# Twenty turns written out, and idle matmuls ahead of ten steps of a two-layer adaLN kernel

## The chip, the cores and the metric

The kernel runs on one core of one Trainium2 chip. The metric is the device time in microseconds (us) of one execution. Three executions without a profiler took 1416.13, 1418.07 and 1418.85 us; the median is 1418.07. All tensors are fp32.

## The reference

The input `x` is 32 sequences of 256 tokens with 128 channels. Two layers follow each other. Each has six modulation vectors per sequence, `silu(c) @ wmod`, and wraps an attention-like block and a feed-forward block:

```
h = layernorm(x) * (1 + ca) + sa ;  x = x + ga * attn(h)
h = layernorm(x) * (1 + cb) + sb ;  x = x + gb * ffn(h)
```

In layer 0 `attn` is linear attention over 32 heads of 4 channels with rotary angles: two decaying states S and K per head are updated token by token (`S = S*beta + phi_k v`, `K = K*beta + phi_k`), the output is a softmax-weighted sum of `phi_q S / (phi_q K + eps)`, then an output product, a residual and a layer norm. In layer 1 `attn` is an RWKV block: layer norm, a shift by one token, key, value and receptance products, a numerically guarded WKV recurrence over the tokens, an output product, and a channel mix (products to 512 channels, relu squared, back to 128, gated). `ffn` in both layers quantizes its input, its weights and its hidden values to FP4 in blocks of 16, and computes `silu(x Wg) * (x Wu)` with 352 hidden channels and the product back to 128.

## The kernel before

The 32 sequences go through as 16 pairs (`PAIRS`); a pair is 512 tokens, four tiles of 128 rows (`NT`). The work of a pair is cut into steps: `a1` to `a8` for the attention of layer 0, `b1` to `b6` for the feed-forward of either layer, `c1` to `c8` for layer 1's attention. A software pipeline runs over turns. In turn n every engine works on pair n (first norm), pair n-1 (layer 0 attention), pair n-2 (layer 0 feed-forward and the first norm of layer 1), pair n-3 (layer 1 attention) and pair n-4 (layer 1 feed-forward). There are 20 turns; turns 0 to 3 fill the pipeline and turns 16 to 19 drain it. The order of the steps within a turn is a list written out by hand for each engine in its `body(n)`. Engines meet through semaphores, and each engine's queue is in order.

The turns are run by the helper `turns` (line 342). Turns 0 to 5 are written out, turns 6 to 15 are a register loop of five iterations with two bodies in each (line 346), and turns 16 to 19 are written out again. Inside the loop the turn number is a register.

Results of TensorE go to eight banks of PSUM. The table `BANK` gives each step's result its bank, so several steps share one. Before a step writes, it waits until the reader of what last stood there is done. The helper `freed` waits for that; `freed_at_ends` waits only when the turn is a plain number, which means that its waits are there in the written-out turns and absent in the loop, where other waits imply them. After these waits a step waits for its data (`after`, `wait_ge`).

Steps that matter below, with the lines of their instructions: `a4d` (L968) sums query times key state into `a_den`; DVE reads it at L1595, inverts it and multiplies in the mix; `a5` (L989) spreads the result over the rows, into the same bank; DVE takes it at L1608 and multiplies the states by it at L1588; `a4` (L977) sums those. `a6` is L1000 and L1001. `b1T_0` and `b1T_1` are transposes through the helper `turn` (L904), as is `c2`; `rows_back` is L1038; `b2` transposes the quantized input (L1096); `b3_0` and `b3_1` are the gate and up products (L1101), in the first use behind the turning of the weights (`turn_weights`, L893 and L897); `b5_0` and `b5_1` transpose the hidden values (L1180) and `down` (L1213) multiplies them. `c3` is L1250 and L1251, `c5` L1271 and L1272, `c6` L1303.

In the profile one fp32 matmul of the program is two records, so `x2` is one matmul.

Of the kernel before, what the change touches and what calls it, by code (L numbers as in the profile page):

```python
# [24 lines left out]
NB, T = 32, 256  # L25
SEQ = 2
TOK = SEQ * T
NT = TOK // P
PAIRS = NB // SEQ
# [63 lines left out]
def after(eng, sem, turn, per_turn=1, nth=None):  # L93

    eng.wait_ge(sem, turn * per_turn + (per_turn if nth is None else nth))
# [16 lines left out]
def freed(eng, sem, turn, per_turn=1, nth=None):  # L112

    if isinstance(turn, int):
        if turn < 0:
            return
        turn = min(turn, PAIRS - 1)
    after(eng, sem, turn, per_turn, nth)


def freed_at_ends(eng, sem, turn, per_turn=1, nth=None):

    if isinstance(turn, int):
        freed(eng, sem, turn, per_turn, nth)
# [12 lines left out]
def build(nc, a, scratch, out):  # L137
    ctx = ExitStack()
    with ctx:
        def sb(name, shape):  # L140
            return ctx.enter_context(nc.sbuf_tensor(name, shape, F32))

        def sem(name):
            return ctx.enter_context(nc.semaphore(name))


        const = sb("const", [P, CONST.shape[1]])

        def cst(k):
            return const[:, CONST_AT[k][0]:CONST_AT[k][1]]  # L150

        ident, center = cst("ident"), cst("center")
# [106 lines left out]
        def bank(name):  # L259
            return ps[:, BANK[name], :]  # L260
# [30 lines left out]
        s_kscan, s_qk_sum, s_den = sem("key_scan"), sem("q_key_sum"), sem("den_mm")  # L291
        s_share, s_shch, s_share_mm, s_qsh = sem("share"), sem("chain_share"), sem("share_mm"), sem("share_times_query")
# [12 lines left out]
        s_fq = [sem(f"ffn_xq{l}") for l in range(2)]  # L305
# [14 lines left out]
        s_wch, s_wexp_in, s_wexp, s_wy = sem("chain_wkv"), sem("wkv_exponents"), sem("wkv_exps"), sem("wkv_y")  # L320
# [20 lines left out]

        def turns(eng, body):

            for n in range(6):
                body(n)
            with eng.Fori(3, PAIRS // 2) as m:
                body(2 * m)
                body(2 * m + 1)
            for n in range(PAIRS, PAIRS + 4):
                body(n)  # L350


# [1 line left out]
        def _(sp):  # L354
# [30 lines left out]
            def body(n):  # L385
                do(load_x, n)
            turns(sp, body)
            for p in range(2):
                sp.wait_ge(s_out[p], 8 * PAIRS)
# [3 lines left out]
        def _(pool):  # L393
# [59 lines left out]
            def body(n):  # L453
# [5 lines left out]
                do(power_a1, n - 2)  # L459
                do(power_a0, n)  # L460
            turns(pool, body)


        @block.scalar
        def _(act):
# [394 lines left out]
            def store(j):  # L860
                act.wait_ge(s_x4, j + 1)
                dst = out_v[j, :, :, :] if isinstance(j, int) else out_v[bass.ds(j, 1), :, :, :].squeeze(0)
                act.dma_start(dst, of_pair(xb, j)).then_inc(s_out[j % 2], 16)
            s.preload_act_table_set("silu_and_others")
            turns(act, body)


        @block.tensor
        def _(pe):
            t_ = nc.tensor  # L870
            n = [0]
# [6 lines left out]
            for l in range(2):  # L878
                for k in range(6):
                    last = t_.matmul(ps_set[l][:, 2, k * NB:(k + 1) * NB], wmod[:, l, k * H:(k + 1) * H], cT[:, l, :],  # L880
                                     start=True, stop=True)
# [7 lines left out]
            def turn_weights(l):  # L889
# [8 lines left out]
                last.then_inc(s_wT, 1)  # L898
                pe.wait_ge(s_wcp, 3 * l + 3)

            def turn(src, dst, ln, i):
                for t in range(NT):
                    after(pe, s_norm[ln], i, NT, t + 1)
                    last = t_.transpose(dst[:, t * P:(t + 1) * P], src[:, t, :], ident)  # L904
                last.then_inc(s_normT[ln], 1)

            def a1(i):
                freed(pe, s_hqc[0], i - 2, 2, 2)
                freed_at_ends(pe, s_outer, i - 1, 2, 2)
                turn(norm[0], bank("a_nT"), "a0", i)  # L910
# [49 lines left out]
                last.then_inc(s_bm_mm, 1)  # L960

            def a4d(i):
                pe.wait_ge(s_qk_sum, i + 1)
                freed(pe, s_hqc[1], i - 3, 2, 2)
                freed_at_ends(pe, s_phi, i, 2, 2)
                for q in range(SEQ):
                    for m in range(M):
                        last = t_.matmul(bank("a_den")[q * 64:(q + 1) * 64, 0:T], cst(f"sel_den{m}"),  # L968
                                         state[:, m, D, q * T:(q + 1) * T], start=(m == 0), stop=(m == M - 1))
                last.then_inc(s_den, 1)  # L970
# [8 lines left out]
                last.then_inc(s_num, 1)  # L979

            def a5(i, q):
                pe.wait_ge(s_share, i + 1)
                if q == 0:
                    freed(pe, s_gd[0], i - 1, SEQ)
                    freed_at_ends(pe, s_shch, i, 2, 1)
                else:
                    freed(pe, s_bm_th, i, 3, 3)
                for m in range(M):
                    last = t_.matmul(bank(f"a_s{q}")[:, m * T:(m + 1) * T], cst(f"spread{m}")[q * 64:(q + 1) * 64, :],  # L989
                                     share[q * 64:(q + 1) * 64, :], start=True, stop=True)  # L990
                last.then_inc(s_share_mm, 1)
# [12 lines left out]
            def a7(i):  # L1004
                freed(pe, s_x4, i - 3)
                freed_at_ends(pe, s_outer, i, 2, 2)
                freed_at_ends(pe, s_hid[0], i - 1, NT, 4)
                freed_at_ends(pe, s_cch, i - 2)
                turn(zn, bank("a_zT"), "z0", i)
# [16 lines left out]
            def b1T_0(i):  # L1026
                freed(pe, s_th[1], i - 2, NT, 3)
                freed_at_ends(pe, s_u, i, SEQ)
                turn(hq[0], bank("f0_nT"), "f0", i)

            def b1T_1(j):
                freed(pe, s_ag, j, SEQ)
                turn(hq[1], bank("f1_nT"), "f1", j)

            def rows_back(l, i):
# [49 lines left out]
                add_columns(bank("c_x3"), acol).then_inc(s_x3mm, 1)  # L1085

            def b2(l, i):
                pe.wait_ge(s_fq[l], i + 1)
                if l == 0:
                    freed(pe, s_hid[1], i - 2, NT, 4)  # L1090
                    freed_at_ends(pe, s_outer, i + 1, 2, 1)
                else:
                    freed(pe, s_yc, i + 2)
                    freed_at_ends(pe, s_hqc[1], i - 1, 2, 1)
                for t in range(NT):
                    last = t_.transpose(bank(f"f{l}_qT")[:, t * P:(t + 1) * P], hq[l][:, t, :], ident)  # L1096
                last.then_inc(s_fqT[l], 1)
# [77 lines left out]
            def hidden_T(l, i, k):  # L1175
                pe.wait_ge(s_hq[l], i + 1)
                for c, (r0, rn) in enumerate(KC):
                    for t in range(2):
                        col = (c % 2) * T + t * P
                        last = t_.transpose(bank(f"f{l}_h{k}{'aac'[c]}")[0:rn, col:col + P], hid[l][:, 2 * k + t, r0:r0 + rn], ident)  # L1180
                last.then_inc(s_hqT[l], 1)
# [13 lines left out]
            def b5_1(j, k):  # L1195
                if k == 0:
                    freed(pe, s_th[0], j + 2, NT, 4)
                    freed_at_ends(pe, s_norm["c1"], j + 1, NT)
                    freed_at_ends(pe, s_th[1], j, NT, 4)
                    freed(pe, s_hid[0], j + 2, NT, 3)  # L1200
                    freed_at_ends(pe, s_fqc[1], j)
                else:
                    freed(pe, s_fth, j + 1)
                    freed_at_ends(pe, s_th[1], j, NT, 1)
                    freed(pe, s_phi, j + 3, 2, 2)
                    freed_at_ends(pe, s_hid[1], j, NT, 2)
                hidden_T(1, j, k)
# [35 lines left out]
            def c2(j):  # L1243
                freed(pe, s_xn[1], j - 1)
                freed_at_ends(pe, s_qsh, j + 1, SEQ, 1)
                turn(norm[1], bank("c_mT"), "b1", j)

            def shifted(dst, k, src):
# [14 lines left out]
                shifted(bank(f"c_{'kvr'[k]}"), k, xs[0]).then_inc(s_kvr, 1)  # L1263

            def c5(j):
                pe.wait_ge(s_wy, j + 1)
                freed(pe, s_th[1], j - 1, NT, 4)
                freed_at_ends(pe, s_outer, j + 2, 2, 1)
                for t in range(NT):
                    dst = bank("c_x")[:, t * P:(t + 1) * P]  # L1270
                    t_.matmul(dst, wy[:, t * P:(t + 1) * P], w_oc[:, :], start=True, stop=False)  # L1271
                    last = t_.matmul(dst, hcol[1][:, t * P:(t + 1) * P], center, start=False, stop=True)  # L1272
                last.then_inc(s_xm_mm, 1)
# [43 lines left out]
            def body(n):  # L1317
# [11 lines left out]
                do(c5, n - 3)  # L1329
                do(c7x, n - 3)  # L1330
                do(layer(b2, 0), n - 2)
                do(b3_0, n - 2, 0)
                do(b3_0, n - 2, 1)
# [12 lines left out]
                do(c6b, n - 3)  # L1346
                do(b5d_1, n - 4, 1)
                do(a4d, n - 1)
                do(c7, n - 3)
                do(b6r_1, n - 4)  # L1350
# [5 lines left out]
                do(b6x_0, n - 2)  # L1356
                do(b6r_0, n - 2)
                do(a5, n - 1, 0)
                do(a5, n - 1, 1)
                do(b1T_1, n - 3)  # L1360
                do(a4, n - 1, 0, 0)
                do(a4, n - 1, 0, 1)
# [528 lines left out]
```

## Time and profile before

| | |
|---|---|
| median of three executions | 1418.07 us (1416.13 to 1418.85) |
| profiled execution, its own time | 1419.27 us |
| its span, first to last instruction | 1417.1 us |
| TensorE busy (PE) | 1199.9 us, 85% |
| DVE busy | 1123.0 us, 79% |
| ACT busy | 1062.4 us, 75% |
| mean granted TensorE clock | 0.928 |
| DMA | 9 GB/s over the span |

The span is cut in 40 slices of 35.4 us in the page; its clock line has one digit for each, in tenths of the full 2.4 GHz. The clock has two levels, 1.2 and 2.4 GHz, so a digit between them is a mean. The idle time in brackets behind an instruction is that of its engine just before it, with what ended it.

### The profile page before, as it was taken

The numbers are of one execution on the slowest core, as the hardware profiler recorded it, in microseconds if no ns is written. First come the engines' busy times: TensorE is split into PE (matmuls) and PEld (weight loads), VectorE is DVE, ScalarE is ACT, GpSimd is POOL, SyncE is SP. The second block draws the span as 40 slices with busy tenths as digits, with TensorE's granted clock in tenths as the row PEclk, the third lists the DMA queues.
The fourth block names the chain that finished last, engine by engine and source line by source line (L and its number), as shares of the span: only waits on it lengthen the run. The fifth ranks groups of instructions, "written<-read, shape, count | busy, mean of one in ns | idle before, by whom it ended". The sixth has DMA issues, their size and how long they took to land.

```text
span 1417.1 us, 19485 instructions
## 1 busy us (share of the span) xinstructions
PE 1199.9 (85%) x5610; PEld 723.4 (51%) x5610; DVE 1123.0 (79%) x1619; ACT 1062.4 (75%) x2849; POOL 219.3 (15%) x286
## 2 busy tenths in 40 slices
PE   5465888989899998989898988999898989978664
PEld 2133364655555564646455554646465555546443
DVE  5838587979889797979798897979698898964523
ACT  5252868789797978797897979797888979687553
POOL 1000203021211212030212111020212121110000
PEclk9576998999999999999999999999899999999686
DMA  4000000000000000000000000000000000000000
GB/s 130 0 1 8 1 3 6 2 15 1 15 1 16 1 15 2 8 8 0 16 0 15 0 15 1 15 0 8 9 0 15 0 15 1 8 1 8 1 8 7
DMA packets 21486, 13.45 MB, mean 9 GB/s; under 512 B 1552, under 2 KB 20624, under 8 KB 21392
## 3 DMA queue, kind: packets, MB, share of 16 engines
q1 hardware_dynamic: 12944, 8.29, 1.9%
q10 hardware_dynamic: 8448, 4.20, 1.0%
q14 instruction: 70, 0.57, 0.1%
q8 instruction: 24, 0.39, 0.1%
HBM read 8.28 MB, written 4.19 MB: 9 GB/s over the span
## 4 chain that ended last, share of the span: by engine, by line
PE 63%; ACT 14%; DVE 12%; issue 8%; POOL 2%; SPq 0%; ACTq 0%; DMA 0%; DVEq 0%; POOLq 0%
PE ps L1101 11%; PE ps L1213 6%; PE ps L1310 4%; PE ps L924 4%; PE ps L1303 4%; PE ps L1180 3%; PE ps L1012 3%; PE ps L1016 3%; PE ps L1250 3%; PE ps L904 3%; PE ps L1251 2%; ACT hq L507 2%; PE ps L977 2%; PE ps L938 2%; POOL rstd_of_a L416 2%
## 5 line engine op out<-in xcount | busy, mean ns | idle before, releaser
L1101 PE MATMUL ps<-wguT,hqcol 128*128 128x352 f32 x512 | 175.4, 485 | 20.5 <-ACT hqcol L681 12.5
L1562 DVE TENSOR_TENSOR_SCAN state<-beta,outer 128x512 f32<-128x512 f32 x128 | 149.2, 1206 | 0.0
L1101 PEld LDWEIGHTS ps<-wguT,hqcol 128*128 128x128 f32 x512 | 97.0, 199 | 82.1 <-issue 30.8
L423 POOL TENSOR_TENSOR var_of_f<-squares_f,eps_sum 128x4 f32<-128x4 f32 x32 | 11.9, 373 | 670.2 <-ACT hq L507 670.2
L1412 DVE SCALAR_TENSOR_TENSOR hid<-hidcol,hid 128x1408 f32<-128x1408 f32 (+1 forms) x68 | 106.2, 1566 | 7.7 <-ACT hidcol L698 7.6
L1213 PE MATMUL ps<-hidcol,wdT 128*128 128x256 f32 (+1 forms) x384 | 94.2, 390 | 0.0
L1634 DVE TENSOR_TENSOR hid<-th,ps 128x352 f32<-128x352 f32 x128 | 63.4, 512 | 32.1 <-PE ps L1101 19.6
L904 PE MATMUL ps<-const,hq 128*128 128x128 f32 x128 | 35.2, 347 | 54.2 <-ACT hq L497 53.3
L977 PE MATMUL ps<-state,const 128*32 128x512 f32 x256 | 73.4, 867 | 7.7 <-DVE state L1588 7.4
L1588 DVE TENSOR_TENSOR state<-state,qshare 128x1024 f32<-128x1024 f32 x64 | 76.8, 1222 | 2.2
L705 ACT ACTIVATE hidcol<-ps 128x512 f32<-128x512 f32 x64 | 38.1, 595 | 51.9 <-PE ps L1180 51.9
L689 ACT ACTIVATE th<-ps 128x352 f32<-128x352 f32 x128 | 58.9, 460 | 24.2 <-PE ps L1101 21.4
L1213 PEld LDWEIGHTS ps<-hidcol,wdT 128*128 128x128 f32 (+1 forms) x384 | 71.6, 196 | 8.9 <-ACT hidcol L707 0.2
L640 ACT ACTIVATE gcol<-ps,mod_cols 128x256 f32<-128x256 f32 x64 | 26.8, 470 | 61.7 <-PE ps L1213 61.2
L1412 DVE SCALAR_TENSOR_TENSOR hq<-xmag,hq 128x512 f32<-128x512 f32 x64 | 44.3, 692 | 33.7 <-ACT xmag L693 31.4
L1180 PE MATMUL ps<-const,hid 128*128 128x128 f32 (+1 forms) x384 | 55.3, 283 | 18.3 <-DVE hid L1413 17.1
L924 PE MATMUL ps<-rope,wqk 128*64 128x512 f32 x256 | 64.5, 626 | 1.7 <-DVE rope L1542 1.7
L1180 PEld LDWEIGHTS ps<-const,hid 128*128 128x128 f32 (+1 forms) x384 | 44.8, 141 | 38.7 <-issue 37.3
L1250 PE MATMUL ps<-xs,w_mixed 128*128 128x512 f32 x96 | 54.4, 650 | 10.3 <-ACT xs L712 10.3
L1303 PE MATMUL ps<-xk,fw_key 128*128 128x512 f32 x128 | 62.6, 602 | 0.0
L1310 PE MATMUL ps<-fw_val,ex 128*128 128x128 f32 x512 | 61.4, 278 | 1.3 <-ACT ex L760 1.3
L1310 PEld LDWEIGHTS ps<-fw_val,ex 128*128 128x128 f32 x512 | 58.4, 192 | 7.3 <-issue 5.0
(234 smaller groups left out, 3246.9 us busy)
## 6 DMA issues: line engine op xcount, KB each, us to landing
xa<-in_x SPq DMA_DIRECT2D x16, 256.0 KB, 2.7
out<-xb ACTq DMA_DIRECT2D x16, 256.0 KB, 2.2
const<-in_const SPq DMA_DIRECT2D x1, 848.0 KB, 6.8
state<-in_wmod SPq DMA_DIRECT2D x1, 768.0 KB, 4.6
outer<-in_wqk SPq DMA_DIRECT2D x1, 256.0 KB, 4.7
ex<-in_w_gate_up SPq DMA_DIRECT2D x2, 128.0 KB, 3.0
fw_key<-in_fw_key SPq DMA_DIRECT2D x1, 256.0 KB, 2.9
fw_val<-in_fw_val SPq DMA_DIRECT2D x1, 256.0 KB, 3.7
```

Source lines behind the costliest of these rows:

```text
L904: last = t_.transpose(dst[:, t * P:(t + 1) * P], src[:, t, :], ident)
L924: ins = t_.matmul(dst[f * 64:(f + 1) * 64, :], wqk[:, k, f, :], rope[:, 2 * f + n_, :], start=(n_ == 0), stop=(n_ == 1))
L977: last = t_.matmul(bank("a_n")[c * NH:(c + 1) * NH, :], cst("sel_num"), state[:, m, c, :], start=(m == 0), stop=(m == M - 1), tile_positio ...
L1101: t_.matmul(bank(f"f{l}_{'gu'[g]}{t}")[:, 0:I_FF], hqcol[l][:, t * P:(t + 1) * P], wguT[:, l, g, :], start=True, stop=True).then_inc(s_gu[ ...
L1180: last = t_.transpose(bank(f"f{l}_h{k}{'aac'[c]}")[0:rn, col:col + P], hid[l][:, 2 * k + t, r0:r0 + rn], ident)
L1213: last = t_.matmul(bank(f"f{l}_d")[:, toks], wdT[0:rn, l, c, :], hidcol[l][0:rn, c, toks], start=(c == 0), stop=(c == 2))
L1250: t_.matmul(dst, w_mixed[:, k, 0, :], src[:, :, 1:T + 1], start=True, stop=False)
L1303: t_.matmul(bank(f"c_f{c}"), fw_key[:, c * P:(c + 1) * P], xk[:, :], start=True, stop=True).then_inc(s_fk_mm, 1)
L1310: last = t_.matmul(bank("c_vk")[:, t * P:(t + 1) * P], fkr[:, c, t * P:(t + 1) * P], fw_val[:, c, :], start=(c == 0), stop=(c == F4 // P - 1))
L1412: return v.scalar_tensor_tensor(dst, mag, low, dst, ALU.max, (ALU.add, ALU.subtract)[part])
L1562: return v.tensor_tensor_scan(state[:, m, c, :], beta[:, m, :], src, 0.0, ALU.mult, ALU.add)
L1588: v.tensor_tensor(state[:, m, 2 * h:2 * h + 2, :], state[:, m, 2 * h:2 * h + 2, :], qshare[:, m:m + 1, :].to_broadcast([P, 2, TOK]), ALU.m ...
```

## The change

The loop of `turns` is replaced by twenty written-out bodies, so the turn number is a plain number everywhere, and `freed_at_ends` waits in all turns. And a helper `run_idle` is added on TensorE. In ten places (a step and a pair) it issues a given number of matmuls of the identity by the first 512 columns of the constants, into the bank that the step is about to write, with `start=True, stop=True`; the step then overwrites them. Each call stands behind the waits for the bank. In `a4d`, `a5`, `b2` and `c5` the wait for the data, which stood first, is moved behind the waits for the bank and behind the call. The numbers are 4 and 7 in `a4d` (pairs 0 and 1), 8 in `a5` (pair 0, first sequence), 4 in `b2` of layer 0 (pair 0), 3 and 5 in `b1T_1` (pairs 14 and 15), 4 in `b2` of layer 1 (pair 15), 9 in `b5_1` (pair 15), 3 in `c2` and 3 in `c5` (pair 15): 50 in all.

```diff
         def turns(eng, body):
 
-            for n in range(6):
-                body(n)
-            with eng.Fori(3, PAIRS // 2) as m:
-                body(2 * m)
-                body(2 * m + 1)
-            for n in range(PAIRS, PAIRS + 4):
+            for n in range(PAIRS + 4):
                 body(n)
...
+            def run_idle(dst, pair, products):
+                for _ in range(products.get(pair, 0)):
+                    t_.matmul(dst, ident, const[:, 0:SEQ * T], start=True, stop=True)
...
             def a4d(i):
-                pe.wait_ge(s_qk_sum, i + 1)
                 freed(pe, s_hqc[1], i - 3, 2, 2)
                 freed_at_ends(pe, s_phi, i, 2, 2)
+                run_idle(bank("a_den"), i, {0: 4, 1: 7})
+                pe.wait_ge(s_qk_sum, i + 1)
...
             def a5(i, q):
-                pe.wait_ge(s_share, i + 1)
                 if q == 0:
                     freed(pe, s_gd[0], i - 1, SEQ)
                     freed_at_ends(pe, s_shch, i, 2, 1)
+                    run_idle(bank(f"a_s{q}"), i, {0: 8})
                 else:
                     freed(pe, s_bm_th, i, 3, 3)
+                pe.wait_ge(s_share, i + 1)
...
             def b1T_1(j):
                 freed(pe, s_ag, j, SEQ)
+                run_idle(bank("f1_nT"), j, {PAIRS - 2: 3, PAIRS - 1: 5})
                 turn(hq[1], bank("f1_nT"), "f1", j)
...
             def b2(l, i):
-                pe.wait_ge(s_fq[l], i + 1)
                 if l == 0:
                     freed(pe, s_hid[1], i - 2, NT, 4)
                     freed_at_ends(pe, s_outer, i + 1, 2, 1)
+                    run_idle(bank("f0_qT"), i, {0: 4})
                 else:
                     freed(pe, s_yc, i + 2)
                     freed_at_ends(pe, s_hqc[1], i - 1, 2, 1)
+                    run_idle(bank("f1_qT"), i, {PAIRS - 1: 4})
+                pe.wait_ge(s_fq[l], i + 1)
...
                     freed_at_ends(pe, s_fqc[1], j)
+                    run_idle(bank("f1_h0a"), j, {PAIRS - 1: 9})
...
             def c2(j):
                 freed(pe, s_xn[1], j - 1)
                 freed_at_ends(pe, s_qsh, j + 1, SEQ, 1)
+                run_idle(bank("c_mT"), j, {PAIRS - 1: 3})
                 turn(norm[1], bank("c_mT"), "b1", j)
...
             def c5(j):
-                pe.wait_ge(s_wy, j + 1)
                 freed(pe, s_th[1], j - 1, NT, 4)
                 freed_at_ends(pe, s_outer, j + 2, 2, 1)
+                run_idle(bank("c_x"), j, {PAIRS - 1: 3})
+                pe.wait_ge(s_wy, j + 1)
```

## Rows read from the trace of the kernel before

**Rows 1.** The page: busy times, clock in 40 slices, chain that ended last.

```profile
PE 1199.9 (85%) x5610; PEld 723.4 (51%) x5610; DVE 1123.0 (79%) x1619; ACT 1062.4 (75%) x2849; POOL 219.3 (15%) x286
...
PEclk9576998999999999999999999999899999999686
...
PE 63%; ACT 14%; DVE 12%; issue 8%; POOL 2%; SPq 0%; ACTq 0%; DMA 0%; DVEq 0%; POOLq 0%
```

**Rows 2.** Windows, turn by turn: stretch, length, busy per engine, clock, DMA share, GB/s.

```profile
346.00:423.20 77.20, 71.56 (x350) 43.24 (x349) 68.28 (x96) 64.46 (x176) 13.96 (x17) 0.98 0.03 8
...
500.70:579.80 79.10, 71.17 (x351) 43.24 (x351) 68.43 (x96) 64.46 (x176) 13.17 (x17) 0.98 0.03 8
579.80:656.90 77.10, 71.39 (x350) 42.98 (x349) 68.08 (x96) 64.22 (x176) 13.88 (x17) 0.98 0.02 7
...
969.40:1050.50 81.10, 73.16 (x351) 43.91 (x351) 68.46 (x97) 64.58 (x176) 13.18 (x17) 0.94 0.02 7
```

**Rows 3.** Timelines of DVE and ACT at one jump: start, us, instruction, idle before.

```profile
544.60 1.23 DVE L1542 TENSOR_TENSOR rope<-hcol,const 128x1024 f32<-128x1024 f32 x1 [2.67 <-issue]
...
543.72 0.78 ACT L712 ACTIVATE xs<-ps,vec 128x512 f32<-128x512 f32 x1 [1.63 <-issue]
```

**Rows 4.** Timeline of PE: 512-column matmuls at the full and at half clock.

```profile
92.24 1.88 PE L938 MATMUL ps<-hcol,wv_rep 128*128 128x512 f32 x4
...
73.43 1.86 PE L950 MATMUL ps<-hcol,wb_rep 128*128 128x512 f32 x2
```

**Rows 5.** Windows of four stretches, for the clock.

```profile
38.00:75.00 37.00, 18.24 (x58) 7.80 (x58) 31.09 (x57) 6.74 (x20) 2.23 (x3) 0.54 0.00 0
...
1232.20:1235.60 3.40, 3.21 (x12) 0.93 (x12) 3.40 (x4) 2.83 (x8) 2.60 (x3) 0.50 0.01 2
...
1385.40:1389.20 3.80, 3.80 (x7) 2.30 (x8) 0.52 (x1) 2.25 (x3) 0.00 (x0) 0.50 0.00 0
...
1403.80:1409.70 5.90, 5.88 (x20) 5.09 (x21) 0.00 (x0) 1.73 (x4) 0.00 (x0) 0.50 0.00 0
```

**Rows 6.** Timeline of PE in turns 1 and 2.

```profile
44.15 1.98 PE L968 MATMUL ps<-state,const 128*64 128x256 f32 x8 [5.15 <-DVE state L1574]
55.20 2.15 PE L989 MATMUL ps<-share,const 64*128 64x256 f32 x8 [9.07 <-DVE share L1602]
...
99.13 1.11 PE L1096 MATMUL ps<-const,hq 128*128 128x128 f32 x4 [5.00 <-DVE hq L1413]
...
104.52 7.32 PE L1101 MATMUL ps<-wguT,hqcol 128*128 128x352 f32 x16 [0.69 <-ACT wdT L491]
...
120.96 1.98 PE L968 MATMUL ps<-state,const 128*64 128x256 f32 x8 [8.54 <-DVE state L1574]
126.52 1.51 PE L1180 MATMUL ps<-const,hid 128*128 128x128 f32 x6 [3.59 <-DVE hid L1413]
```

**Rows 7.** Timeline of DVE in turns 1 and 2.

```profile
50.37 0.42 DVE L1595 TENSOR_SCALAR share<-ps 128x256 f32<-128x256 f32 x1
...
57.31 1.29 DVE L1608 TENSOR_TENSOR qshare<-ps,qk 128x512 f32<-128x512 f32 x2
...
114.30 0.63 DVE L1547 SCALAR_TENSOR_TENSOR qk<-ps,eqk 128x512 f32<-128x512 f32 x1
```

**Rows 8.** Timeline of PE in turns 17 to 19.

```profile
1319.30 1.16 PE L904 MATMUL ps<-const,norm 128*128 128x128 f32 x4 [3.08 <-ACT norm L538]
...
1342.33 0.80 PE L1271 MATMUL ps<-w_oc,wy 128*128 128x128 f32 x2 [3.29 <-DVE wy L1705]
...
1374.62 1.54 PE L904 MATMUL ps<-const,hq 128*128 128x128 f32 x4 [5.45 <-ACT hq L497]
...
1383.48 1.12 PE L1096 MATMUL ps<-const,hq 128*128 128x128 f32 x4 [5.03 <-DVE hq L1413]
1385.38 6.88 PE L1101 MATMUL ps<-wguT,hqcol 128*128 128x352 f32 x16 [0.78 <-ACT hqcol L681]
1403.82 2.80 PE L1180 MATMUL ps<-const,hid 128*128 128x128 f32 x12 [11.56 <-DVE hid L1413]
```

## Prediction

> **What bounds the kernel now.** I read the page first: the busy times, the clock line and the chain of waits [rows 1]. TensorE carries 63% of the chain that ended last, ACT 14%, DVE 12%, and 8% is "issue". TensorE is busy 85% of the span, but the clock line shows 5 to 7 in some of the first slices and 6, 8, 6 in the last three, and 8 or 9 in between. So three places have to be read apart: the middle, where the loop is, the first two turns, and the last two.
>
> The middle I read by windows, cut where TensorE starts the first product with `fw_key` in each turn [rows 2]. A turn inside the loop takes 77.1 us with TensorE busy for about 71.5. Every second one takes more: 79.1, 79.2, 79.0 and 81.1, of which the first and the last stand in the rows. These are the four turns in which the register loop jumps back. The timelines at one jump show why [rows 3]: DVE stands still for 2.67 us and ACT for 1.63 us, both put down to "issue", which is to say that nothing the profile shows was missing. The written-out turn just before the loop (346.0 to 423.2) is as fast as one inside an iteration.
>
> **Turns written out.** Removed: four jumps. Against 77.1 they cost 2.0 + 2.1 + 1.9 + 4.0 = 10.0 us. The last has a second low stretch of the clock in it (0.94 against 0.98), which could fall elsewhere again, so I take 9.5. Added: the waits that the helper `freed_at_ends` leaves out inside the loop, and eight more bodies of code. Turn 5 [rows 2] has both and takes 77.20, so they cost 0 to 0.1 per turn, at most 1 for ten turns. They lie beside TensorE's queued work; without that cover every one of the ten turns would pay. Bounds: -10.0 to -7; value -9.5.
>
> The Trainium skill's page "Runtime: NRT & Kernel Launch", section "Instruction fetch mechanics", has a rule that speaks a little against this part: code is fetched in blocks of 16 KiB, and each new block costs something, though mostly hidden. By it the ten turns, all new code now, would give back a part; the measured 77.20 against 77.10 leaves room for 1 us in all, and the sum goes by that.
>
> **The price of one product.** A product is the identity by 512 columns of fp32. Two matmuls of 512 columns (x4 records) took 1.88 us, with a tail of about 0.16, at the full clock, so one is 0.86; one (x2 records) took 1.86 at half clock, so 1.71 [rows 4]. Fifty are added: 43 us at the full clock, 86 at half. All ten blocks stand ahead of a wait for data but behind the waits for the bank, so two things count: the overshoot past the data, and the clock that the work behind them finds. In the rows it took 3.8 us of unbroken work until the clock rose in one place and 5.9 in another, and it is low for nearly all of 38 to 75, where TensorE has long gaps [rows 5].
>
> **The first turns** [rows 6, 7]. *a4d, pair 0, 4 products.* TensorE waits 5.15 us until 44.15. Even if the four start only in the middle of this gap and run at half clock (6.8 us), they and L968's 1.98 us end at about 50.4, and the result is first read by DVE's L1595 at 50.37. Cost 0.
>
> *a5, pair 0, 8 products.* Idle 9.07 us until 55.20, but the bank is that of `a_den`, which comes free when L1595 ends at 50.8. TensorE was idle from 46.1, so the clock is low then: two products at 1.71, the rise after some 3.7 us, the other six at 0.86, end at 59.4, 4.2 us after the data. On DVE L1608 took the share at 57.31; now it gets it at 60.1. That is +2.8 us on DVE's chain, with nothing of DVE's own to fill it (all products warm: +0.5; a late rise: +4). Behind it TensorE waits for DVE's L1588 with gaps again, so the work up to 75 may see the low clock as before; if it didn't, L989 and the eight small matmuls of L1000 and L1001 (as many columns as two products) would give back 1.0 + 1.7. I take +2.8; bounds -2 to +4.
>
> *b2, layer 0, pair 0, 4 products.* Idle 5.00 us until 99.13; the products run warm from 94.1 to 97.5, in time. Then come short steps with gaps between them and the 16 records of L1101 that took 7.32 us; by the price eight matmuls of 352 columns take 8 x 352/512 x 0.86 = 4.7. All warm this saves 2.6, and some 1.5 more in the three short steps of L1096's kind (1.11). I expect the clock to fall once among the short steps and take -2.2, which goes on to DVE's chain for the hidden blocks. Bounds -4.1 to 0.
>
> *a4d, pair 1, 7 products.* Idle 8.54 us until 120.96, the bank free when L1547 ends at 114.9. Seven products take 6.0 warm, 7.7 with a low stretch: 0 to 2 us late. The gap of 3.59 us ahead of L1180 hides this and lets the clock fall again. Value -0.3; bounds -2.5 to +1. First turns together: +2.8 - 2.2 - 0.3 = +0.3, between -6 and +4.
>
> **The last turns** [rows 8]. *b1T_1, pair 14, and c2, pair 15, 3 products each.* The first three run warm, but each transpose behind them is paced by ACT: -0.2. The next three start at 1316.2 (1319.30 less 3.08) at half clock and end between 1319.5 and 1321.3, against data at 1319.30; the two products of 512 columns in `c3` behind them then take 1.7 and not 3.4: -1.0 (bounds -1.9 to +2.0).
>
> *c5, pair 15, 3 products.* Idle 3.29 us until 1342.33, 2.6 us of products. The eight matmuls behind (two products' columns) take 1.7 and not 3.4, and ACT's squares hang on their end: -1.7, less 0.4 for a fall of the clock shortly after: -1.3 (bounds -1.9 to +0.5).
>
> *b1T_1, 5, and b2, layer 1, 4 products, pair 15.* Idle 5.45 and 5.03 us; the products take 4.3 and 3.4 and end before the data. The transposes between them shorten by about 0.5, L1096 from 1.12 to 0.6, L1101 from 6.88 to 4.7: 3.3, of which I leave 0.4 for ACT, which has table loads between its silus. Value -2.9 (bounds -4 to +1).
>
> *b5_1, pair 15, 9 products.* Idle 11.56 us until 1403.82. Nine products take 7.7, and some 3.6 us of idle time are left in which the clock can fall again; the 5.9 us at half clock that follow [rows 5] would be 2.95 warm. Value -0.6 (bounds -2.9 to +1). Last turns: -0.2 - 1.0 - 1.3 - 2.9 - 0.6 = -6.0, between -11 and +2.
>
> **Sum.** -9.5 + 0.3 - 6.0 = -15.2 us. The profiled execution took 1419.27 (span 1417.1, 2.2 us around it); the median shown is 1418.07, 1.2 less, so 1402.9.
>
> **Rivals.**
> (1) The products don't hold the clock where the work is. For it: behind most blocks stand transposes and gaps, and from 1232.2 TensorE was busy 3.21 of 3.40 us with transposes and narrow matmuls at 0.50 [rows 5]. Against it: dense L1101 did get the clock back. Then the blocks of pair 15 in b1T_1, b2 and b5_1 give 2 and not 3.5, those in c2 and c5 0.7 and not 2.5, b2 of pair 0 nothing, and a5 stays at +2.8: -9.5 + 2.8 - 2.7 = -9.4, 1408.7. The Trainium skill's page "TensorE: Matmul & The Clock Gate", Part 4 ("PE-mode transpose"), speaks for this rival: transposes, it says, don't count towards the full clock. The stretch just named agrees, but it holds narrow matmuls too and so proves nothing.
> (2) The clock holds better than I think, in the first turns too (a5 at 0, b2 at -4, a4d at -1; last turns -9): -9.5 - 5 - 9 = -23.5, 1394.6. For it: the products fill just those waits behind which the clock was low. Against it: gaps are left behind every block.
> (3) Writing the turns out gives nothing, since straight code stops DVE and ACT as often as the jumps did, or the added waits bind: 0 + 0.3 - 6.0, 1412.4. Against it is turn 5 at 77.20.
> (4) Slower: the products run at half clock, 1.71 each, because each block begins after idle time. Then a5's eight end at 64.5 (7.2 us late for DVE), b2's four at 100.9 (+1.8), a4d's seven at 126.9 (+1), c2's at 1321.3 and c5's at 1344.2 (+4 together), the last three blocks come 3, 2 and 4 late: 23 us of overshoot and nothing gained, against 9.5: about 1432. It decides once the overshoots sum to more than 9.5 us. Against it: the clock came within 3.8 to 5.9 us even after the longest gaps.
>
> **How the numbers follow.** Forecast 0.50, (1) 0.23, (2) 0.17, (3) 0.06, (4) 0.04. The forecast's own range is 1399 to 1407. With two in ten left out I reach to both neighbours: 1395 to 1410. A measurement of this kernel tells about 0.2%, 2.8 us, from no change. Faster by more: all but (4) and the tail of (3), 0.95; within 0.2%: 0.02; slower: 0.03.
>
> **What would show it.** In the profile after, the turns from 4 to 16 take 77.1 to 77.5, and DVE has no stop of 2.67 us. L989 starts near 59.5 and L1608 near 60; if it starts before 58.5, a5's term is wrong. The first L1101 block takes under 6.3 us, the last one about 5, and the eight matmuls of L1271 and L1272 of pair 15 about 1.9. The prediction is wrong if every second turn still takes 79, if a turn in the middle grows, or if L1101 and L1180 of pair 15 keep their 6.88 and 2.80.

## Result and the profile after

The changed kernel took 1399.26 us (median of four runs, 1395.93 to 1402.27) against 1418.46 for the kernel before on the same chip (four runs): a ratio of 0.9866, interval 0.9838 to 0.9895, 19 us less. The forecast was 1402.9, with a range of 1395 to 1410. The profiled execution took 1395.93, span 1394.0, so its trace shows 23.1 us less than that of before, 4 us more than the medians do. A trace is one execution; two places where executions of the same code differ are read below (turn 3, and the last turns).

The page of the changed kernel, to be held against [rows 1]:

```profile
PE 1228.5 (88%) x5710; PEld 732.2 (53%) x5710; DVE 1121.0 (80%) x1619; ACT 1062.6 (76%) x2849; POOL 222.7 (16%) x286
...
PEclk9888999999999999999999999999999999989899
...
q8 instruction: 49, 0.80, 0.2%
q14 instruction: 47, 0.39, 0.1%
...
PE 67%; ACT 12%; DVE 11%; issue 6%; POOL 3%; SPq 0%; DMA 0%; ACTq 0%; DVEq 0%; POOLq 0%
```

Slices 2 to 4 of the clock line go from 5, 7, 6 to 8, 8, 8, and the last three from 6, 8, 6 to 8, 9, 9. TensorE is busy for 28.6 us more in a shorter span; the fifty added products alone take 52.2 us, so the rest of its work got shorter. The page counts 100 records more, all of L898, the products' line. The two instruction queues moved in opposite ways: q8 from 24 packets (0.39 MB) to 49, q14 from 70 to 47. Straight code seems to be fetched on the one, and code after a jump on the other: the run with two jumps (e7) lies between, at 36 and 59.

The windows of the changed kernel, cut at the same instruction as in [rows 2] (now L1310): a turn in the middle that was hit by nothing, and the longest one.

```profile
343.20:420.00 76.80, 71.43 (x350) 43.23 (x349) 68.02 (x96) 64.36 (x176) 13.98 (x17) 0.98 0.03 8
...
804.30:881.80 77.50, 72.14 (x351) 43.66 (x351) 68.11 (x96) 64.48 (x176) 13.98 (x17) 0.96 0.03 8
```

Where the loop jumped, DVE now goes on without a stop; its timeline at the same step as in [rows 3] (L1549, no idle time before it):

```profile
537.29 0.69 DVE L1420 TENSOR_TENSOR hq<-hq,xblk 128x512 f32<-128x512 f32 x1
537.89 1.22 DVE L1549 TENSOR_TENSOR rope<-hcol,const 128x1024 f32<-128x1024 f32 x1
```

Where the profiled 23.1 us went, by the start of the first fw_key product of a turn, before and after:

| stretch | before | after | change |
|---|---|---|---|
| start to turn 3 | 189.6 | 188.9 | -0.7 |
| turn 3 to 4 | 79.6 | 77.4 | -2.2 |
| turn 4 to 16 | 935.5 | 923.3 | -12.2 |
| turn 16 to 17 | 77.9 | 78.1 | +0.2 |
| turn 17 to 18 | 70.4 | 66.6 | -3.8 |
| turn 18 to the end | 64.1 | 59.7 | -4.4 |

TensorE's timeline in the first turns (against [rows 6]):

```profile
39.90 5.40 PE L898 MATMUL ps<-const 128*128 128x512 f32 x8 [1.45 <-DVE qk L1554]
45.22 1.09 PE L968 MATMUL ps<-state,const 128*64 128x256 f32 x8
50.30 8.83 PE L898 MATMUL ps<-const 128*128 128x512 f32 x16 [3.98 <-DVE share L1602]
59.06 1.14 PE L990 MATMUL ps<-share,const 64*128 64x256 f32 x8
62.89 1.05 PE L977 MATMUL ps<-state,const 128*32 128x512 f32 x4 [2.69 <-DVE state L1595]
...
96.81 3.60 PE L898 MATMUL ps<-const 128*128 128x512 f32 x8
101.97 0.66 PE L1100 MATMUL ps<-const,hq 128*128 128x128 f32 x4 [1.56 <-DVE hq L1420]
...
105.93 5.00 PE L1105 MATMUL ps<-wguT,hqcol 128*128 128x352 f32 x16 [0.69 <-ACT wdT L486]
...
125.62 1.50 PE L1184 MATMUL ps<-const,hid 128*128 128x128 f32 x6 [2.55 <-DVE hid L1420]
```

The eight products of a5 stand from 50.30 to 59.1, past the data, and L990 follows at once. DVE waits for it, which it did not before (against [rows 7]):

```profile
54.16 0.43 DVE L1609 TENSOR_TENSOR share<-share,mixp 128x256 f32<-128x256 f32 x1
54.51 2.33 DVE L1569 TENSOR_TENSOR_SCAN state<-beta,outer 128x512 f32<-128x512 f32 x2
60.22 1.29 DVE L1615 TENSOR_TENSOR qshare<-ps,qk 128x512 f32<-128x512 f32 x2 [3.38 <-PE ps L990]
```

And the last turns (against [rows 8]):

```profile
1300.92 3.90 PE L898 MATMUL ps<-const 128*128 128x512 f32 x6
1304.65 0.60 PE L903 MATMUL ps<-const,norm 128*128 128x128 f32 x4
...
1322.01 2.84 PE L898 MATMUL ps<-const 128*128 128x512 f32 x6
1325.34 0.49 PE L1278 MATMUL ps<-w_oc,wy 128*128 128x128 f32 x2 [0.49 <-DVE wy L1712]
...
1359.39 4.53 PE L898 MATMUL ps<-const 128*128 128x512 f32 x8
1364.64 0.66 PE L1100 MATMUL ps<-const,hq 128*128 128x128 f32 x4 [0.72 <-DVE hq L1420]
1366.08 4.97 PE L1105 MATMUL ps<-wguT,hqcol 128*128 128x352 f32 x16 [0.78 <-ACT hqcol L676]
1371.79 7.96 PE L898 MATMUL ps<-const 128*128 128x512 f32 x18 [0.74 <-issue]
1382.98 1.53 PE L1184 MATMUL ps<-const,hid 128*128 128x128 f32 x12 [3.23 <-DVE hid L1420]
1384.90 2.83 PE L1218 MATMUL ps<-hidcol,wdT 128*128 128x256 f32 x12 [0.39 <-ACT hidcol L702]
```

Each block ends before its data but that of c2, whose transposes follow at once. L1105 went from 6.88 to 4.97 us, L1184 from 2.80 to 1.53: the full clock was there.

### The profile page after: what moved, and what is told of

Its sections match the earlier page's. It is cut to its first block, busy times and chain, and to the rows that moved or that the text cites. A ratio compares the mean times of both kernels' runs of the same rounds, so it can differ in the third digit from the quotient of the medians.

```text
span 1394.0 us, 18809 instructions
## 1 busy us (share of the span) xinstructions
PE 1228.5 (88%) x5710; PEld 732.2 (53%) x5710; DVE 1121.0 (80%) x1619; ACT 1062.6 (76%) x2849; POOL 222.7 (16%) x286
## 4 chain that ended last, share of the span: by engine, by line
PE 67%; ACT 12%; DVE 11%; issue 6%; POOL 3%; SPq 0%; DMA 0%; ACTq 0%; DVEq 0%; POOLq 0%
PE ps L1105 10%; PE ps L1218 6%; PE ps L1317 4%; PE ps L923 4%; PE ps L1310 4%; PE ps L1184 3%; PE ps L1017 3%; PE ps L1256 3%; PE ps L1013 3%; PE ps L903 3%; PE ps L1257 3%; ACT hq L502 2%; PE ps L977 2%; PE ps L937 2%; POOL rstd_of_a L411 2%
## 5 line engine op out<-in xcount | busy, mean ns | idle before, releaser
L1105 PE MATMUL ps<-wguT,hqcol 128*128 128x352 f32 x512 | 168.2, 470 | 20.4 <-ACT hqcol L676 12.5
L1105 PEld LDWEIGHTS ps<-wguT,hqcol 128*128 128x128 f32 x512 | 93.1, 191 | 78.2 <-issue 24.6
L1218 PE MATMUL ps<-hidcol,wdT 128*128 128x256 f32 (+1 forms) x384 | 92.5, 384 | 0.4 <-ACT hidcol L702 0.4
L977 PE MATMUL ps<-state,const 128*32 128x512 f32 x256 | 70.9, 831 | 8.8 <-DVE state L1595 8.4
L1595 DVE TENSOR_TENSOR state<-state,qshare 128x1024 f32<-128x1024 f32 x64 | 76.8, 1221 | 2.2
L903 PE MATMUL ps<-const,hq 128*128 128x128 f32 x128 | 34.8, 335 | 48.7 <-ACT hq L492 47.4
L1218 PEld LDWEIGHTS ps<-hidcol,wdT 128*128 128x128 f32 (+1 forms) x384 | 70.5, 193 | 8.9 <-ACT hidcol L702 0.6
L1310 PE MATMUL ps<-xk,fw_key 128*128 128x512 f32 x128 | 62.6, 602 | 0.0
L1184 PE MATMUL ps<-const,hid 128*128 128x128 f32 (+1 forms) x384 | 54.1, 278 | 8.7 <-DVE hid L1420 7.7
L937 PE MATMUL ps<-hcol,wv_rep 128*128 128x512 f32 x128 | 60.5, 595 | 0.0
L898 PE MATMUL ps<-const 128*128 128x512 f32 x100 | 52.2, 676 | 8.7 <-DVE qk L1554 4.0
```

Of the source, the lines that this page charges most:

```text
L937: ins = t_.matmul(two_banks(("a_v1", "a_v0")[h])[:, n_, :], wv_rep[:, c, :], hcol[0][:, :], start=True, stop=True)
L977: last = t_.matmul(bank("a_n")[c * NH:(c + 1) * NH, :], cst("sel_num"), state[:, m, c, :], start=(m == 0), stop=(m == M - 1), tile_positio ...
L1105: t_.matmul(bank(f"f{l}_{'gu'[g]}{t}")[:, 0:I_FF], hqcol[l][:, t * P:(t + 1) * P], wguT[:, l, g, :], start=True, stop=True).then_inc(s_gu[ ...
L1218: last = t_.matmul(bank(f"f{l}_d")[:, toks], wdT[0:rn, l, c, :], hidcol[l][0:rn, c, toks], start=(c == 0), stop=(c == 2))
L1310: t_.matmul(bank(f"c_f{c}"), fw_key[:, c * P:(c + 1) * P], xk[:, :], start=True, stop=True).then_inc(s_fk_mm, 1)
L1595: v.tensor_tensor(state[:, m, 2 * h:2 * h + 2, :], state[:, m, 2 * h:2 * h + 2, :], qshare[:, m:m + 1, :].to_broadcast([P, 2, TOK]), ALU.m ...
```

## Experiments

Runs of one kernel spread over 2 to 11 us, and the kernel before had medians of 1416.1 to 1421.6 on the chips used. Times are compared by the ratio to the kernel before on the same chip; terms of a few us are read in the traces, one execution each, which can be far from the median: that of e1 took 1399.55, 5 us below it. "First start" is that of the first fw_key product.

**e1, turns only; e2, products only.**

```diff
 e1: run_idle(...) with {} in all ten places
 e2: the loop of turns kept; run_idle issues only where the pair is a plain number
```

> Only the turns are written out; no idle product is issued. Theory A (the jumps were the cost): the four jumps cost 10 us, and each of the ten turns becomes some 0.2 us shorter because the register instructions are gone; 11 to 12 us less than before, 1406.5 to 1407.5, every turn from 4 to 16 at 76.8 to 77.2, last turns as before (64 us from the last start of the fw_key products to the end). Rival B (the writing-out gained mainly through the clock, since low stretches fell elsewhere once the products had moved the turns): then it gives 8 us or less, 1410 or more, and turns with 77.5 to 78.5 appear.

> The loop is kept and all fifty products are issued, with the moved data waits. Theory A: the two parts add up, so this gives what the last turns gave, 7 to 8 us less than before, 1410.5 to 1411.5, and DVE still has four stops of about 2.6 us. Rival C (the products gain only because the written-out turns put the ends at another phase of the clock): 3 us or less, above 1415.

Measured: e1 1404.89 (six runs), ratio 0.9919 (0.9897 to 0.9941); e2 1412.99 (twelve runs), ratio 0.9968 (0.9951 to 0.9985); before 1418.32. By the medians that is 13 and 5 us, by the ratios 11.5 (8.4 to 14.6) and 4.5 (2.1 to 6.9). The product of the two ratios is 0.9887, inside the interval of the changed kernel, so the parts add up within the noise. e1 came out as theory A says, and B's 8 us or less falls. e2 missed: A's 7 to 8 us lies outside its interval, and C's 3 us or less lies inside. It is the trace that speaks against C: from turn 16 to the end e2, with its loop, takes 204.2 us, and the changed kernel 204.4. In e1 the turns from 4 to 16 take 76.8 to 77.4 us. In e2 the four turns with a jump take 80.6, 79.4, 80.9 and 79.0, those inside an iteration 77.2, and DVE stops as before:

```profile
541.16 1.23 DVE L1554 TENSOR_TENSOR rope<-hcol,const 128x1024 f32<-128x1024 f32 x1 [2.48 <-issue]
```

**e3, products in the first turns only; e4, in the last only** (turns written out in both).

```diff
 e3: b1T_1, b2 of layer 1, b5_1, c2, c5 with {}
 e4: a4d, a5, b2 of layer 0 with {}
```

> Turns written out, products only in the first two turns (a4d 4 and 7, a5 8, b2 of layer 0 4). Theory A: as e1 within 1 us, since the 2.8 us that a5's overshoot costs are paid back by b2 of layer 0; the start of the first fw_key products moves from 189.6 to about 189. Rival D (the first blocks carry a good part of the gain): 3 to 5 us less than e1.

> Turns written out, products only in the last two turns. Theory A: 7 to 8 us less than e1, the same as the changed kernel within 1 us, about 1399.5; the time from the last start of the fw_key products to the end falls from 64 to about 60. Rival D: 3 us or more above the changed kernel.

Measured: e3 1406.29, ratio 0.9924 (0.9902 to 0.9946); e4 1396.94, ratio 0.9869 (0.9840 to 0.9898). The first turns' products are worth nothing beside e1's 0.9919, the last ones' 8 us by the medians and 7 by the ratios (an estimate from the two intervals: 2 to 12), and e4 with 27 products equals the changed kernel with 50. The last stretch, from turn 18 on, is 63.4 us in e1 and 59.7 in e4.

**e5, without a5's eight; e6, with sixteen.**

```diff
-                    run_idle(bank(f"a_s{q}"), i, {0: 8})
+                    run_idle(bank(f"a_s{q}"), i, {})          (e5)
+                    run_idle(bank(f"a_s{q}"), i, {0: 16})     (e6)
```

> The changed kernel without the eight products of a5 (pair 0); the other 42 stay. Theory A (the eight overshoot their data and hold DVE's chain back by 2.8 us, which b2 of layer 0 pays back): the share is multiplied at 57.3 again, L1105's first block still ends 3 to 4 us earlier than without products, and the first fw_key products start near 186.0, against 188.9 in the changed kernel: about 3 us less, 1396.5. Rival E (the eight warm the clock for what follows and so are worth having): the start of the fw_key products is at 189 or later and the time the same or more.

> The changed kernel with sixteen products in a5 (pair 0) in place of eight. Theory A: eight more at the full clock, 0.86 each, all overshoot: the first DVE multiplication by the share moves from 60.2 to about 67.1 and the first fw_key products from 188.9 to about 195 (up to 1 us less where the clock stays up longer). Rival E: less than 4 us later, because the work behind finds the full clock.

Measured: e5 1399.84, ratio 0.9847 (0.9827 to 0.9868); e6 one run of 1409.54. In the traces the first start is 186.0 in e5, 188.9 in the changed kernel and 197.0 in e6. In e5 L990 stands at its old place and takes its old, cold time; in e6 the products hold TensorE until 67:

```profile
54.95 2.17 PE L990 MATMUL ps<-share,const 64*128 64x256 f32 x8 [8.42 <-DVE share L1609]
```

```profile
57.03 1.29 DVE L1615 TENSOR_TENSOR qshare<-ps,qk 128x512 f32<-128x512 f32 x2
```

```profile
50.97 16.10 PE L898 MATMUL ps<-const 128*128 128x512 f32 x32 [5.60 <-DVE share L1602]
67.00 1.14 PE L990 MATMUL ps<-share,const 64*128 64x256 f32 x8
```

The dose goes as theory A says, 2.9 us for the first eight and 8.1 for the next (6.9 by price; part of the rest is that e6's first turn began 0.6 later). Counted from the moment the share is ready (the end of L1609), L1615 starts 2.2 us later in e5, 5.6 in the changed kernel and 12.9 in e6: 3.4 us for the first eight and 7.3 for the next. E falls. The trace settles the term; the times don't: 0.9847 and 0.9866 lie within each other's intervals.

**e7, two jumps in place of four.**

```diff
-            for n in range(6):
+            for n in range(10):
                 body(n)
-            with eng.Fori(3, PAIRS // 2) as m:
+            with eng.Fori(5, PAIRS // 2) as m:
```

> The kernel before with turns 6 to 9 written out too, so that the loop has three iterations and jumps back twice; no products. Theory A (each jump costs about 2.0 to 2.5 us): half of the gain of e1, 5 to 6 us less than before, about 1412.5, with two turns of 79 us and the rest at 76.8 to 77.2. Rival F (the loop costs something as such, once, or by its register instructions in every turn): the gain is 4/10 of e1's or less at the same two long turns, or the jumps that are left cost more.

Measured: 1408.96 (four runs) against 1421.64, ratio 0.9913 (0.9893 to 0.9933), 12.4 us; that is as much as e1 and twice what was expected. The trace says less: its span is 8.7 us shorter than that of the kernel before. The turns written out take 76.8 to 77.2, those inside iterations 77.1 and 78.1, and the two with a jump 80.0 and 79.2, so 2 to 3 more; DVE's stops there are 2.47 and 2.43 us. So each jump costs its 2 to 3 us also here. But from turn 4 to 16 the trace gains 4.5 us (935.5 to 931.1) where e1 gains 12.5, which is rival F's 4/10 or less and not half. The other 4.3 us lie from turn 16 to the end, 208.1 against 212.4, where the instructions are the same and the clock fell elsewhere (see the last turns below). The median of e7 is lower than all this explains, and F is not settled; both stay open (the kernel before was 3 us slower on this chip than on the others).

**e8, three products per turn.** In the middle TensorE stands idle 2.77 us ahead of b1T_1, and once per turn, in all but a few turns, the clock falls for 3.4 us behind that (449.9 to 453.3 in the changed kernel). The first two lines are the changed kernel's, the third is e8's at the place of the second:

```profile
447.69 1.39 PE L903 MATMUL ps<-const,hq 128*128 128x128 f32 x4 [2.77 <-ACT hq L492]
...
451.71 1.83 PE L977 MATMUL ps<-state,const 128*32 128x512 f32 x4 [0.35 <-DVE state L1595]
```

```profile
452.61 1.05 PE L977 MATMUL ps<-state,const 128*32 128x512 f32 x4 [0.80 <-DVE state L1595]
```

```diff
 (from e4)
-                run_idle(bank("f1_nT"), j, {PAIRS - 2: 3, PAIRS - 1: 5})
+                run_idle(bank("f1_nT"), j, {**{k: 3 for k in range(PAIRS - 1)}, PAIRS - 1: 5})
```

> e4 (turns written out, products only in the last two turns) with three products ahead of b1T_1 in every pair, in the idle 2.77 us in which the clock falls once per turn. Rival G (the low stretch of 3.4 us in each turn costs half of itself): 1.7 us less for each of 13 turns, 22 us, about 1375. Theory A': in the traces a turn with a low stretch takes 76.8 to 76.9 us and the one turn without one (from 266.3 to 343.2 in the changed kernel) takes 76.8 too, so what stands there isn't on the path: the same as e4 within 2 us, 1395 to 1399, with the low stretches gone or moved.

Measured: 1397.29, ratio 0.9834 (0.9815 to 0.9852). Windows of 1000 us and of one turn:

```profile
189.80:1190.00 1000.20, 945.83 (x4581) 569.00 (x4580) 884.29 (x1236) 835.54 (x2287) 182.04 (x221) 1.00 0.03 8
...
420.70:497.50 76.80, 72.98 (x356) 43.97 (x355) 68.05 (x96) 64.34 (x176) 13.97 (x17) 1.00 0.03 8
```

The clock is at 1.00 through the whole middle, and the turn still takes 76.8 us. What it brings is that no turn from 4 on is longer than 76.9, where the changed kernel has some of 77.1 to 77.5: 1.0 us from turn 4 to 16 (923.3 to 922.2). G falls. The clock's mean over the span was no measure of what it cost: the stretch holds short work between waits for DVE and ACT, and what the full clock saves there turns up as waiting (L977 waits 0.80 us for DVE in e8, 0.35 in the changed kernel).

**e11, six per turn.**

```diff
 (from e8)
-  {k: 3 for k in range(PAIRS - 1)}
+  {k: 6 if k < PAIRS - 2 else 3 for k in range(PAIRS - 1)}
```

> e8 with six products in place of three ahead of b1T_1 in pairs 0 to 13: 2.6 us more TensorE work per turn, past the data. If TensorE's queue is what sets the turn just behind this place, each of 13 to 14 turns grows by 2.3 to 2.6 us, 30 to 36 us in all, to about 1430. If the turn has slack there (which would be why a half-clock stretch of 3.4 us cost nothing), it grows by less than 1 us per turn.

Measured: one run of 1401.47. A turn takes 77.1 to 77.2 us against 76.8: 0.3 us more for 2.6 us of work.

```profile
446.18 5.42 PE L898 MATMUL ps<-const 128*128 128x512 f32 x12
451.43 0.60 PE L903 MATMUL ps<-const,hq 128*128 128x128 f32 x4
451.96 1.07 PE L977 MATMUL ps<-state,const 128*32 128x512 f32 x8
```

Here L903, 1.49 us when ACT paced it, runs through in 0.60, since ACT had finished meanwhile. That is slack of the kind which made the low stretches free.

**e10, without b5_1's nine.**

```diff
-                    run_idle(bank("f1_h0a"), j, {PAIRS - 1: 9})
```

> The changed kernel without the nine products ahead of b5_1 (pair 15). If b5_1's term was as small as forecast (0.6), the last stretch, from L1184's start to the end, stays at 11 to 11.6 us and the time within 1 us of the changed kernel. Theory H (the nine hold the clock and carry most of the gain at the very end): L1184 takes 2.8 and L1218 4.4 us again, the stretch takes 13.3 us as before the change, 2.3 us more in all.

Measured: 1398.87 against 1416.13, ratio 0.9870 (0.9837 to 0.9903).

```profile
1384.69 2.79 PE L1184 MATMUL ps<-const,hid 128*128 128x128 f32 x12 [12.03 <-DVE hid L1420]
1387.27 4.24 PE L1218 MATMUL ps<-hidcol,wdT 128*128 128x256 f32 x12
```

From L1184 to the end 13.1 us pass, against 11.0 with the nine and 13.3 in the kernel before. Between these two traces the nine are worth 2.1 us, as theory H says; they are not worth that in every execution (see the last turns below). The times again can't tell 2 us.

**e9, combined.**

```diff
 (from e8)
 a4d: {1: 7}    b2 of layer 0: {0: 4}
 b5_0, first half, behind its bank waits:
+                    run_idle(bank("f0_h0a"), i, {0: 3})
```

> e8 with the blocks of the first turns that were worth having: b2 of layer 0 (4) and a4d of pair 1 (7) but not a4d of pair 0 and not a5, and three products more ahead of b5_0 of pair 0, in the idle 4.25 us before L1184. Theory A: the first fw_key products start at about 186.0 as in e5, less 1.5 to 2.5 us for the hidden transposes and down products of pair 0, which then find the full clock: 183.5 to 184.5; turns at 76.8; last turns as in e8. About 5 us less than e8 on the same chip, 19 in all over the first version of the products' middle: a ratio of about 0.980. Rival E: the first turns stay at 189 whatever stands in them, ratio 0.984 to 0.986.

Measured: 1394.43 (five runs, 1389.39 to 1395.54), ratio 0.9827 (0.9798 to 0.9855). The first start is 184.9, the lowest of all. L1184 takes 0.87 and not 1.50, and what follows is warm:

```profile
118.28 2.84 PE L898 MATMUL ps<-const 128*128 128x512 f32 x6
122.51 0.87 PE L1184 MATMUL ps<-const,hid 128*128 128x128 f32 x6 [1.39 <-DVE hid L1421]
...
125.51 2.86 PE L1219 MATMUL ps<-hidcol,wdT 128*128 128x256 f32 x12 [0.28 <-DVE share L1603]
```

The three products bring 1.1 us of the 1.5 to 2.5 expected. This is the lowest ratio measured, 22 us below the kernel before on its chip; that it beats the changed kernel (0.9866) is not shown, since the intervals overlap.

**The first turns, read across the runs.** The first start has a spread of its own, from the start-up: 187.7 to 189.8 in the six traces without products in these turns. Counted from the end of the first L1609 (L1602 in the kernel before) to the first fw_key product, these six take 134.4 to 134.8 us, e5 131.2 and e9 130.2. The four with all 23 products of the first turns take 134.3 (changed kernel), 134.9 (e3), 135.3 (e2) and 137.7 (e10). e10 runs the same instructions there; it met the low clock at other places, among them the block behind b2's four products, which took 5.00 in the other three:

```profile
107.14 6.48 PE L1105 MATMUL ps<-wguT,hqcol 128*128 128x352 f32 x16 [0.69 <-ACT wdT L486]
```

**The last turns, read across the runs.** The traces without the 27 products, then those with all of them (e10 lacks the nine of b5_1):

| | turn 16 to the end | last L1105 block | c5's eight matmuls (L1278, L1279) | L1184 to the end |
|---|---|---|---|---|
| before | 212.4 | 6.88 | 3.78 | 13.3 |
| e3 | 211.2 | 6.69 | 3.75 | 13.2 |
| e7 | 208.1 | 7.50 | 2.05 | 11.9 |
| e1 | 208.0 | 7.43 | 2.02 | 11.9 |
| e6, e9 | 208.2, 208.6 | 4.97 | 2.05 | 13.2 |
| e5, e8, e11 | 206.0, 205.4, 206.8 | 4.97 | 2.05 | 11.0 |
| changed, e2, e4 | 204.4, 204.2, 204.4 | 4.97 | 2.05 | 11.0 |
| e10 | 206.4 | 4.97 | 2.05 | 13.1 |

The last L1105 block is short in every trace that has the products ahead of it. c5's eight matmuls were as short in e1 and e7 without any product. And in e6 and e9 the nine products were there, with the same 3.23 us of idle time behind them, and the clock fell all the same, so that L1184 took 2.82 and not 1.53 us. c5's first matmul in e1, then the end of e9:

```profile
1325.35 0.46 PE L1278 MATMUL ps<-w_oc,wy 128*128 128x128 f32 x2 [3.38 <-DVE wy L1712]
```

```profile
1379.98 2.82 PE L1184 MATMUL ps<-const,hid 128*128 128x128 f32 x12 [3.23 <-DVE hid L1421]
1382.60 4.36 PE L1219 MATMUL ps<-hidcol,wdT 128*128 128x256 f32 x12
```

The means of the two groups, 209.9 and 206.0, lie 3.9 us apart, less than the 7 to 8 of the times; the traces are single executions, and the two groups overlap by half a microsecond.

**Turn 3 to 4, read across the runs.** This turn takes two values: 77.4 us in the changed kernel, e1, e2, e4, e8, e9 and e10, and 79.3 to 79.7 in the kernel before, e3, e5, e6, e7 and e11. Windows of the kernel before, then of the changed kernel, then of e11:

```profile
189.60:269.20 79.60, 69.56 (x326) 41.03 (x325) 66.77 (x94) 63.11 (x174) 14.45 (x17) 0.94 0.02 4
```

```profile
188.90:266.30 77.40, 67.16 (x325) 39.67 (x325) 66.68 (x95) 62.94 (x174) 14.44 (x17) 0.98 0.02 4
```

```profile
187.70:267.00 79.30, 71.83 (x337) 42.28 (x336) 66.77 (x94) 62.83 (x174) 14.44 (x17) 0.98 0.02 4
```

The mean clock doesn't tell them apart (0.98 in e11). The place does: in the six slow ones the clock is low for 3.4 us beginning 46 us behind the turn's start, in none of the fast ones. Dense products stand there, the first use of the turned weights; the same four records in the kernel before, in the changed kernel and in e11:

```profile
235.41 2.64 PE L1101 MATMUL ps<-wguT,hqcol 128*128 128x352 f32 x4 [0.69 <-ACT wdT L491]
```

```profile
234.19 1.45 PE L1105 MATMUL ps<-wguT,hqcol 128*128 128x352 f32 x4 [0.69 <-ACT wdT L486]
```

```profile
233.23 2.44 PE L1105 MATMUL ps<-wguT,hqcol 128*128 128x352 f32 x4 [0.69 <-ACT wdT L486]
```

A half-clock stretch earlier in this turn cost nothing: with one of 3.4 us (changed kernel) and with none (e8, e9) the turn takes 77.4. The low stretch at the dense products costs about 2 us. In this turn the changed kernel's gain of 2.2 is luck of one execution: e3 and the changed kernel run the same instructions up to turn 17, and one took 79.7 and the other 77.4.

## Why the prediction was right, step by step

**Turns written out: -9.5 forecast, 11.5 by e1's ratio (13 by its median), 12.2 in the trace.** The jumps were the main cause: 10.0 us in the kernel before, 11 in e2, and no stop of DVE without them. The step "they cost 0 to 0.1 per turn" failed: written-out turns are not dearer but cheaper, 76.8 to 76.9 against 77.1 to 77.2 inside the loop, 2 us over the ten turns. I took it from turn 5, one turn at 77.20, while the turn ahead of it had 76.8; one sample was too few, and that window (346.0 to 423.2) ends at a product of turn 6, inside the loop. Why they are cheaper is not shown: in e7 turns 7 and 8, written out too, took 77.1 and 77.2. Rival (3) is refuted.

**First turns: +0.3 forecast, no gain in e3.** The -0.7 of the table is the start-up; counted from L1609 the changed kernel gains 0.1 and e10 loses 3. a5 costs about what was forecast (+2.8; 2.9 by the first start, 3.4 where DVE waits), with L1615 at 60.22 for the "60.1" of the working. b2's -2.2 was too small where the clock held through the short steps: L1105 took 5.00, and from the start of L1100 to the end of L1105 8.96 us passed against 12.71: -3.7. The clock did "fall once", as the forecast had it, in e10, at L1105 itself. a4d of pair 1 (-0.3) gave nothing, because L1184 still met the low clock. So the small sum came out though each term was off: a5 cost up to 0.6 more, b2 gave 1.5 more, and that these cancel is luck.

**Last turns: -6.0 forecast, 7 to 8 us in e4.** The sum was right, its parts less so. *c2* (-1.0): the two products of `c3` behind it took 1.98 against 2.95 to 3.48, in every trace that has the block: -1.0 to -1.5. *c5* (-1.3): the eight matmuls took 2.05 against 3.78 in the kernel before, but 2.02 in e1 without a product, so the block is worth up to 1.7 us in some executions and nothing in others. *b1T_1 and b2 of pair 15* (-2.9): -2.1 from the end of c8's matmuls to L1184 (32.5 us in all eight traces with every block of the last turns, 34.5 to 35.3 in the four without); this is the surest term. *b5_1* (-0.6): the working left "some 3.6 us of idle time" in which "the clock can fall again". 3.23 us were left. In six of eight traces the clock stayed, and L1184 to the end took 11.0 us, against 11.9 to 13.3 in the five traces without the nine: 0.9 to 2.3 us. In e6 and e9 it fell, and with 13.2 nothing was gained. The mechanism was right; the mean over the traces is -1.1.

**The rest.** Rival (1) is refuted at the last L1105 block in every trace with products there, and at L1184 and L1218 in six of eight. Rival (2), -9 in the last turns and -5 in the first: the kernel's own trace shows -8 in the last, the times 7 to 8, so it was no further off there than the forecast; its part on the first turns did not come true, as a5's overshoot shows. Rival (4) is refuted: three of the ten blocks overshot by more than 1 us, a5 and the two of a4d, and behind a4d nobody waited. The brackets given for the two groups (-6 to +4 and -11 to +2) are narrower than the sums of their terms' bounds (-8.6 to +5 and -10.9 to +4.3); nothing was decided by that.

## What to carry to other kernels

Idle matmuls pay where TensorE's work behind a wait is long, dense and what the end hangs on, and where the block ends before the data; count from when its bank comes free, not from when TensorE stops, and take them away where they overshoot. Where idle time is left behind a block, the clock may fall in it in one execution and not in the next, so a single trace does not tell what such a block is worth. A low clock is worth repairing only where the stretch is not paced by another engine: look at what the turn takes with and without it before adding work. Loops in a kernel with several busy engines should be judged by what each engine does at the jump.

## What the runs showed of the hardware

At each of the ten jumps back in the three traces with a loop (kernel before, e2, e7) DVE stood still for 2.4 to 2.7 us and ACT for 1.6 to 1.9. The two instruction queues carried 24 or 25 and 70 packets with four jumps, 36 and 59 with two, 48 to 50 and 47 or 48 with none, and no written-out turn was dearer for it. In the middle the turns with a half-clock stretch of 3.4 us took no longer than the one without (76.8 and 76.9), while one of the same length over dense products in turn 3 cost about 2. And the same code with the same 3.23 us of idle time kept the full clock in six executions and lost it in two.
